# Two products of a recurrent step, alternated block by block, with the pieces of x passed through DRAM

## What is computed

```
def cell(h, x):
    gi = x @ W_ih + b_ih
    gh = h @ W_hh + b_hh
    r, z = sigmoid(i_r + h_r), sigmoid(i_z + h_z)
    n = tanh(i_n + r * h_n)
    return (1 - z) * n + z * h
hs = scan(cell, cond, x over T)
y = x + ffn(hs)     # gate, up, silu, down; each operand rounded to fp8
```

## Time and profile before

| what | value |
|---|---|
| median of three runs | 3157.83 us |
| span of the profiled execution, first to last instruction | 3161.0 us |
| TensorE busy | 2796.5 us (88% of the span) |
| VectorE busy | 1810.4 us (57%) |
| GpSimd busy | 1223.7 us |
| ScalarE busy | 1176.4 us |
| time given to the change's stages (0 to 2305.2 us) | 73% of the span |

### The profile page before, as it was taken

The page is one execution under the profiler, slowest core; times in us unless marked ns, Lnnn a source line. Parts: engine busy times, 40 slices in busy tenths (PEclk is TensorE's granted clock), DMA queues, the critical chain, the costliest instruction groups (busy, mean ns, idle before and its releaser), DMA issues. The chain is left out here.

```text
span 3161.0 us, 156688 instructions
## 1 busy us (share of the span) xinstructions
PE 2796.5 (88%) x67963; PEld 1879.9 (59%) x67963; DVE 1810.4 (57%) x3503; ACT 1176.4 (37%) x2417; POOL 1223.7 (39%) x600
## 2 busy tenths in 40 slices
PE   5799999999988989999999999999921699999996
PEld 2378876887776868887767655647410244444442
DVE  8635223522488634426739154270966488888887
ACT  2422222222211122225609122130345477777774
POOL 0156555655544545652160523416020133333333
PEclk9899999999999999999999999999965899999998
DMA  7812222222212212223454442424240222332221
GB/s 218 275 52 65 62 60 55 64 63 56 57 52 54 59 47 62 66 61 93 139 132 141 125 135 91 133 79 139 87 158 28 87 78 81 91 87 84 85 74 49
DMA packets 212035, 286.41 MB, mean 91 GB/s; under 512 B 46893, under 2 KB 171847, under 8 KB 211719
## 3 DMA queue, kind: packets, MB, share of 16 engines
q1 hardware_dynamic: 194663, 235.99, 26.6%
q10 hardware_dynamic: 13568, 33.56, 3.0%
q0 software_dynamic: 3680, 15.21, 1.7%
HBM read 226.10 MB, written 58.48 MB: 90 GB/s over the span
## 5 line engine op out<-in xcount | busy, mean ns | idle before, releaser
L871 PE MATMUL psum<-whole_w,whole_hot 64*32 64x384 f16 x32768 | 1206.7, 326 | 40.8 <-issue 17.0
L879 PE MATMUL psum<-low_w,low_hot 64*32 64x384 f16 x16384 | 1009.7, 326 | 3.5 <-issue 3.5
L871 PEld LDWEIGHTS psum<-whole_w,whole_hot 64*32 64x32 f16 x32768 | 743.4, 92 | 200.9 <-DVE whole_w L1053 52.2
L753 POOL TENSOR_TENSOR low_hot<-low_a,sum_mask 128x1024 f16<-128x1024 f16 x256 | 485.2, 1895 | 534.3 <-DVE low_a L1041 433.0
L747 POOL TENSOR_TENSOR whole_hot<-whole_a,whole_mask 128x2048 f16<-128x2048 f16 x128 | 462.4, 3612 | 581.0 <-PE psum L871 511.6
L1053 DVE TENSOR_SCALAR whole_w<-psum 32x384 f16<-32x384 f32 x496 | 272.2, 549 | 702.2 <-PE psum L871 694.2
L821 ACT ACTIVATE whole_w<-psum 32x384 f16<-32x384 f32 x496 | 239.3, 482 | 969.8 <-PE psum L871 966.9
L941 PE MATMUL psum<-low_w,low_hot 64*64 64x384 f16 x12288 | 507.2, 325 | 9.5 <-ACT low_hot L839 7.9
L941 PEld LDWEIGHTS psum<-low_w,low_hot 64*64 64x64 f16 x12288 | 372.6, 108 | 143.3 <-ACT low_hot L839 8.4
L879 PEld LDWEIGHTS psum<-low_w,low_hot 64*32 64x32 f16 x16384 | 406.8, 92 | 61.6 <-issue 8.2
L1828 PE MATMUL psum<-wh,hT 128*64 128x256 f32 (+1 forms) x1856 | 315.2, 492 | 0.0
(11 more groups left out here) (265 smaller groups left out, 3086.0 us busy)
## 6 DMA issues: line engine op xcount, KB each, us to landing
low_w<-w_rows SPq DMA_DIRECT2D x384, 144.0 KB, 2.5
low_w<-w_rows SPq DMA_DIRECT2D x256, 120.0 KB
whole_w<-w_rows SPq DMA_DIRECT2D x1024, 24.0 KB, 1.8
x_gates<-x_out ACTq DMA_DIRECT2D x58, 384.0 KB, 2.4
xg<-x_gates SPq DMA_DIRECT2D x58, 384.0 KB, 3.2
low_w<-w_rows SPq DMA_DIRECT2D x256, 72.0 KB
low_w<-w_rows SPq DMA_DIRECT2D x384, 48.0 KB, 2.3
w_rows<-w_split SPq DMA_DIRECT2D x24, 384.0 KB, 6.5
```

The lines of the kernel that those rows point to most:

```text
L753: nc.gpsimd.tensor_tensor(low_hot[:, buf].rearrange("p (s k) b -> p s k b", s=SUBS), low_a[:, bass.ds(c, 1), :, :].rearrange("p a s b -> p ...
L871: last = nc.tensor.matmul(run[m][u][j * Q:(j + 1) * Q, :], whole_hot[rows[u], buf, sign, kk, j % 2 * Q:(j % 2 + 1) * Q], whole_w[rows[u], ...
L879: nc.tensor.matmul(run[m][u][j * Q:(j + 1) * Q, :], low_hot[rows[u], buf, kk, j % 2 * Q:(j % 2 + 1) * Q], low_w[rows[u], buf, at:at + UC], ...
```

## The change

The products now stand in `STAGES`: {(0,0), (0,1)}, {(2,0)}, {(1,0), (1,1)}, {(3,0)}, {(2,1)}, {(3,1)}, {(4,1)}, {(5,1)}. In a stage of two, blocks of x and of the state alternate: block c of x, block c of the state, block c+1 of x, and so on. Each product has one of the two buffers. Both column halves take every term together, so a block has 16 terms. A base is made while the other product's block runs.

The pieces of x for steps 0 to 3 and of the first state no longer pass through `pick`. They are turned in the setup, cut by VectorE, written to a DRAM tensor `pieces` (5 DMAs of 3072 runs of 128 bytes), and read back onto their partitions: 16 DMAs of 8 partitions with 64 runs of 128 bytes each for `low_a`, and 8 with 32 runs for `whole_a`, an operand of a two-level product. For x of step 0 and the first state ScalarE issues them in the setup (48 in all). For x of steps 2, 1 and 3 SyncE issues them between its weight loads (16, 24 and 16).

The plain x sums leave the setup. There are four windows of 7, 7, 7 and 8 pairs, beside the gates of steps 2 to 5. The gates of step 0 run beside (2,0), those of step 1 beside (3,0), none is woven into a two-level product. The load of `w_x` moves from the start of the exact steps to the start of (3,0).

The diff, cut to its core:

```diff
-X_FINE, H_FINE = 2, 2
+FINE = 2
-PRODUCTS = ((0, 0), (0, 1), (1, 0), (1, 1), (2, 0), (2, 1), (3, 0), (3, 1), (4, 1), (5, 1))
-CUT_FROM = 5
+STAGES = (((0, 0), (0, 1)), ((2, 0),), ((1, 0), (1, 1)), ((3, 0),), ((2, 1),), ((3, 1),), ((4, 1),), ((5, 1),))
-SOLO = 3
-WEAVE = 10
-            SETUP_PAIRS = 7
-            WINDOWS = EXACT - X_SUMS + 1
+            WINDOWS = EXACT - FINE
+            pieces = nc.dram_tensor("pieces", [X_SUMS + 1, A_KINDS, D, B], F16, kind="Internal").ap()
+            def put_pieces(eng, operand, split_a):
+                eng.dma_start(pieces[operand].rearrange("a (g p) b -> p a g b", p=P),
+                              split_a.rearrange("p a (g b) -> p a g b", b=B)).then_inc(pieces_out, 16)
+            def load_low(eng, operand, kinds, slot):
+                for r, kind in enumerate(kinds):
+                    for u in range(2):
+                        at = u * B + r * SK
+                        eng.dma_start(low_a[at:at + SK, slot].rearrange("k c s b -> k (c s) b"),
+                                      pieces[operand, kind].rearrange("(n k) b -> k n b", k=SK)).then_inc(rows_of_in[slot], 16)
+            def load_whole(eng, operand, m, slot):
+                ... (2 parts x 2 subs x 2 kinds, 8 partitions with 32 runs each)
 setup, ScalarE, after chunk n of the weights:
-                            if n == 0: ... place_bias, copy_rows
-                            elif n <= SETUP_PAIRS: ... take_out, place_bias, copy_rows
+                            if n == 0:
+                                for j, operand in enumerate((0, H0)):
+                                    a.wait_ge(first_cut, CUTS * (j + 1))
+                                    put_pieces(a, operand, first_split[:, j])
+                            elif n == 1:
+                                a.wait_ge(pieces_out, 32)
+                                for j, (operand, slot) in enumerate(((0, ROWS_X0), (H0, ROWS_H))):
+                                    load_low(a, operand, LOW_ROWS, slot)
+                                    load_whole(a, operand, j, slot)
 setup, VectorE, ahead of the first chunk:
+                        for j, src in enumerate((turned_x[0], turned_h0)):
+                            for _ in cut(v, cut_link, src, scale[:, 2 + j:3 + j], first_rest[:, 0], first_rest[:, 1],
+                                         [first_split[:, j, kind] for kind in range(A_KINDS)]):
+                                pass
 exact steps, SyncE:
+                        for c in range(2):
+                            for m in range(2):
+                                load(0, m, c, m)
+                            if c == 0:
+                                for n, t in enumerate(LATER):
+                                    sp.wait_ge(later_cut, CUTS * (n + 1))
+                                    put_pieces(sp, t, later_split[n])
+                        sp.wait_ge(pieces_out, 16 * (2 + len(LATER)))
+                        load_low(sp, 2, SUM_ROWS, ROWS_X2)
+                        pair_blocks(sp, pair_load(0), 2)
+                        for c in range(BUFS):
+                            load(2, 0, c, sum_buf(c))
+                            if c == 1:
+                                sp.wait_ge(hot_ok, block_no(2, 0, 0) + 1)
+                                load_low(sp, 1, LOW_ROWS, ROWS_X0)
+                                load_whole(sp, 1, 0, ROWS_X0)
+                        sum_blocks(sp, sum_load(2, 0), BUFS, BUFS)
+                        for m in range(2):
+                            load(1, m, 0, m)
+                        sp.wait_ge(hot_ok, block_no(1, 0, 0) + 1)
+                        load_low(sp, 3, SUM_ROWS, ROWS_X2)
+                        store_state(0)
+                        pair_blocks(sp, pair_load(1), 1)
 exact steps, TensorE:
-                                    for kk in range(SOLO):
-                                        term(first + kk, 0)
-                                    based(1, ready)
-                                    for kk in range(SOLO, BK):
-                                        term(first + kk, 0, ((first + kk - SOLO, 1),))
-                                    for kk in range(BK - SOLO, BK):
-                                        term(first + kk, 1)
+                            def term(m, kk):
+                                for u in range(2):
+                                    add_whole(m, u, 1, kk)
+                                for u in range(2):
+                                    add_low(m, u, kk)
+                                for u in range(2):
+                                    last = add_whole(m, u, 0, kk)
+                            with pe.Fori(0, NBK) as c:
+                                for m in range(2):
+                                    ... (waits for bases, weights, one-hots of this block)
+                                    for kk in range(BK):
+                                        term(m, kk)
+                        for t in range(FINE):
+                            if t > 0:
+                                turn(t)
+                                pick(t)
+                            ... (clear)
+                            pair_chain(t)
+                            sum_chain(t + FINE, 0)
+                        for t in range(FINE, EXACT):
+                            turn(t)
+                            ... (clear)
+                            pick(t)
+                            sum_chain(t, 1)
+                            x_window(t)
```

More of the change, by code:

```diff
@@ L643, in renewals, with stage_of, first_block @@
-                def renewals(eng, renew):
-                    with eng.Fori(0, NBK // PAIR - 1) as n:
-                        for b in range(PAIR):
-                            renew(n * PAIR + (b + 1), (b + 1) % PAIR)
-                    renew(NBK - 1, (NBK - 1) % PAIR)
+                def stage_of(t, m):
+                    return next(n for n, stage in enumerate(STAGES) if (t, m) in stage)
+                def first_block(n):
+                    return sum(NBK * len(stage) for stage in STAGES[:n])
@@ new lines, in sum_blocks, with pair_blocks @@
+                def sum_blocks(eng, block, first=0, done=0):
+                    for c in range(done, first):
+                        block(c, sum_buf(c))
+                    with eng.Fori(first // BUFS, NBK // BUFS) as n:
+                        for j in range(BUFS):
+                            block(n * BUFS + j, sum_buf(j))
+                def pair_blocks(eng, block, first, last=NBK):
+                    with eng.Fori(first, last) as c:
+                        for m in range(2):
+                            block(c, m)
@@ new lines, in _ @@
+                        for half in range(2):
+                            sp.dma_start(state[half * B:(half + 1) * B, :], cond[:, half * HALF:(half + 1) * HALF]).then_inc(h0_in, 16)
+                        with nc.allow_non_contiguous_dma(reason="index columns, 6 KB"):
+                            sp.dma_start(dcol[:], dn_idx.rearrange("(c p) -> p c", p=P)).then_inc(dcol_in, 16)
+                        for c in range(2):
[5 more added lines that the diff above has]
+                                    put_pieces(sp, t, later_split[n])
@@ L781, in x_window @@
+                        for j in range(2):
+                            load_rows(a, j)
                         def x_window(t):
@@ L796, in x_window, with place @@
                                     copy_rows(a, n // 2 + 1, WINDOW_BANKS)
+                        def place(t):
+                            for n in range(places(t)):
+                                a.wait_ge(selected, placed_by(t) + n + 1)
+                                group, whole = pick_of(t, n)
+                                if whole:
+                                    last = nc.scalar.activation(whole_a[Q:2 * Q, 1, group::PB, :], picked(n, slice(Q, 2 * Q)), ACT.Copy)
+                                else:
+                                    for part in range(2):
+                                        last = nc.scalar.activation(low_a[part * B:(part + 1) * B, ROWS_H, group::PB, 0, :], picked(n, slice(0, B)), ACT.Copy)
+                                last.then_inc(placed, 1)
@@ L1037, in place_second @@
+                        def place_second(t):
+                            for n in range(places(t)):
+                                v.wait_ge(selected, placed_by(t) + n + 1)
+                                group, whole = pick_of(t, n)
                                 if whole:
-                                    last = nc.vector.tensor_copy(whole_a[B + Q:2 * B, group::PB, :], picked(n, slice(B + Q, 2 * B)))
+                                    last = nc.vector.tensor_copy(whole_a[B + Q:2 * B, 1, group::PB, :], picked(n, slice(B + Q, 2 * B)))
@@ L1383, in build @@
+                        for t in range(FINE, EXACT):
+                            cut_state(t)
+                            place_second(t)
```

(4 more changed lines are left out.)

663 lines of the change are left out of this document (321 added, 342 removed).

## The result

| | before | after |
|---|---|---|
| median of the runs, us | 3159.05 (3154.62 to 3167.09) | 3081.42 (3077.94 to 3084.92) |
| ratio, 95% interval | | 0.9747 (0.9729 to 0.9766) |
| span of the profiled execution, us | 3161.0 | 3078.3 |

2.5% faster; 3027 us was forecast, in a range of 2960 to 3115. Of the experiments' executions one, of e2_lag_back, took 4275.01 us at a granted clock of 0.642 (its nine others 0.929 to 0.931), and no ratio uses it. Against the span that the prediction added up, 3030.1, the profile is 48.2 us longer. First the windows of the profile after, cut where TensorE changes from one stage to the next. Columns: stretch in us, its length, busy time of each engine with its instructions, granted clock of TensorE as a share of full speed, mean busy share of the 16 DMA engines, GB/s.

A forecast was written before the change was run, and what follows sets the result against it. TensorE's chain of products and gaps bounds the kernel. 187.4 + 38.1 + 63.9 + 9 - 82.2 - 2 = 214.2 us gained, less 83.3 for small DMAs, takes span 3161.0 to 3030.1, median 3027 us; range 2960 to 3115.

The forecast's parts named there:

- p: Time one DMA of 512 runs of 128 bytes holds its issuing queue: 1.15 us taken, ends 0.5 and 4.1.
- Part 1, no lag: Two-level products: a block falls from 19 steps to 16, 9.27 to 7.81 us, 187.4 us gained over 128 blocks.
- weights can't keep 7.81: Rival, pair blocks: weight loads come late, a block takes 8.3 us, 64 us more, 3091 us; chance 0.08.
- at 0.52 a block is 8.3 us: Rival, pair blocks: steps with two halves don't keep 0.49 us when they follow one another, about 3091 us; chance 0.04.
- Part 2, the order: Gains between and within products: 38.1 us from woven gates, 63.9 from gaps, 9 from two starts fewer.
- Part 3, the x sums: Setup gets back nearly nothing; step 2's gates need their own window, 82.2 us lost; w_x load ahead of (3,0), 2 lost.
- Part 4, DRAM: Pieces' DMAs in setup, first stage, (2,0) and second stage: 92p - 22.5, 83.3 us lost.
- cheap rival: Small runs cost no more than the issue, p = 0.5: 24 us lost, 2968 us; chance 0.22.
- 20p - 7.9: Loss in (2,0) from 24 DMAs of pieces ahead of block 2's weight load: 15.1 us.
- 14 us for sharing engines with w_rows: Setup: ScalarE, held 40p by its 48 DMAs, is held 14 us more by nine writes of w_rows.
- dear p: Rival: small runs as dear as behind dcol beside w_x, p = 2.2: 180 us lost, 3123 us; chance 0.12.
- slower rival: ScalarE and SyncE held until small runs have landed, p = 4.1, setup first: 355 us lost, 3298 us; chance 0.06.

The follow-up runs named there:

- e2_lag_back: The kernel after with half 1 of each block again three terms behind half 0 (19 steps), TensorE alone changed: 3170.94 us, ratio to before 1.0024.
- e3: The kernel before with the lag set to 0, blocks of one product still following each other: 3326.85 us, ratio to before 1.0527.
- e4: The kernel after with 7 waits instead of 9 at a pair block's start, low weights' wait moved behind 16 matmuls: 3068.16 us, ratio to before 0.9713.
- e7: The kernel after with seven pairs of plain x sums back in the setup, 22 left for the four windows: 3068.57 us, ratio to before 0.9703.
- e8: The kernel after with the pair products' loop written out twice (4 blocks in its body) on TensorE: 3638.65 us, ratio to before 1.1501.
- e1: The kernel after with the pair products' loop written out four times (8 blocks in its body) on TensorE: 3552.15 us, ratio to before 1.1248.
- e5: The kernel after with low rows' DMAs reading 8 runs of 8192 bytes instead of 512 short ones, same bytes: 3045.29 us, ratio to before 0.9619.

## Why the prediction was right, and by how much its terms were off

| term | forecast, us | measured, us | miss |
|---|---|---|---|
| end of the setup | 191 | 177.7 | -13.3 |
| setup's end to first pair block | 14.1 | 14.5 | +0.4 |
| first stage | 521 | 549.0 | +28.0 |
| (2,0) | 101.2 | 100.5 | -0.7 |
| turn, cut and pick ahead of the second stage | 18 | 22.9 | +4.9 |
| second stage | 506 | 528.7 | +22.7 |
| (3,0), (2,1) with their gaps | 189.2 | 194.4 | +5.2 |
| four windows against three and the gates | 82.2 | 83.3 | +1.1 |

The 189.2 is what the prediction leaves of before: a gap of 0.5, 86.0 for (3,0), 2 for the load of w_x, a gap of 14.0, and 86.7 for (2,1) (the window 1570.20:1656.90 of before).

The range was right and so was the sign. But 3081.42 us lies above the forecast's own part of the range, 2995 to 3078, though p came out at 1.1, and two of the prediction's own signs stand against each other: the setup with VectorE idle for 35 to 45 us and the two holes came, and so did "blocks over 8 us", which it lists under wrong. That the sum ended only 48 us off is luck in part: the setup was put 13.3 us too high and the pair stages 50.7 too low.

Point by point:

- **Part 1, no lag: right in sign, mis-sized, and the largest miss.** "16 steps at 0.488, 7.81 us, if the supplies keep up": steps and supplies are as forecast, but at a boundary TensorE waited for itself. The same branch, register operations and waits stand in before, at steps of one half; the prediction took 9.27 us there as 19 steps and nothing else. The rows of before hold two errors that cancel: across a block's change half 1's last low pass (shown below the list) and half 0's first one, 320.85 in the earlier trace rows, are 0.71 us apart, 0.22 more than a step, and half 1 ends 1.21 us behind half 0, 0.25 less than three steps. By the windows, parts 1 and 2 gave 128.0 us, with 17.8 us of holes of the first stage in them, where 187.4 and 9 for the starts were claimed. e2 shows that the split was wrong too: 41 us are the order's, 87 the lag's once the order is there, and by e3 the lag's removal alone is a loss. The rival "weights can't keep 7.81" named this size of block, 8.3 us, and another cause; e4 speaks against that cause. The rival "at 0.52 a block is 8.3 us" named it too, and the steps of 0.49 us speak against that one.
- **Part 2, the order: right.** No gates in a pair stage, a gap of 0.4 us ahead of (2,0). The gap ahead of the second stage was put 4.9 us too low. The one ahead of (3,0) is 5.1 us, not 0.5 and 2 for w_x: TensorE waits 4.6 us for `low_hot`, which ScalarE begins at 1396.13, behind the four issues of w_x.
- **Part 3, the x sums: right for the windows, 83.1 us each.** That the setup gets "nearly nothing" back holds less well once ScalarE and its DMAs fill it: in e7 the pairs cost it 17 us.
- **Part 4, DRAM: right in size, in part by luck.** p was 1.04 to 1.25 for 1.15, a value taken as the middle of two that differ by a factor of four. In the first stage DMAs cost 10.7 and 4.4 us for 15.7, but the 4.4 are behind the three writes of pieces, for which the sum has no term: by it the loads ahead of the 16 DMAs end 21.3 us into the stage, and they ended at 31.7. (2,0) has 15.5 for 15.1, the second stage none for 2.0. The hole of 2.7 us, by the instructions' first fetch, was in no term either. One slip in the cheap rival: by 20p - 7.9 its (2,0) costs 2.1 us, not 4.1. The 14 us for sharing engines with w_rows in the setup did not appear: 48 DMAs held ScalarE 43.2 us, not 46 + 14. That term, drawn from bytes at 245 GB/s, was the other mis-sized one (ScalarE came to them at 78.5 instead of 72, and was let go 10 us sooner than reckoned); with it the setup hid a quarter of the first miss.

The row for part 1, of before:

```profile
320.14 0.35 PE L879 MATMUL psum<-low_w,low_hot 64*32 64x384 f16 x4
```

The low p and the dear p are both refuted. The slower rival is as well: ScalarE was let go as soon as its 48 issues were through.

## What to carry to other kernels

A lag that covers a dependence can cost less than its steps (here 0.68 us for three steps of 0.49), because its ragged ends overlap and hide the boundary's own instructions; price its removal with the boundary laid bare, here about 0.1 us for each two semaphore waits and 0.5 us for a loop end. Many small DMAs behind one another hold the engine that issues them: give them out between its other work, or to the queue with slack, before changing anything else. Count writes as well as reads when DMAs are put into a queue. Before writing a loop out, multiply its instructions by 64 bytes: 98 KB stayed here, 197 KB was fetched in every pass.

## What the runs showed of the hardware, unexpected

- A loop body on TensorE of 1536 matrix instructions (98 KB) runs from what is held; one of 3072 is fetched in each pass, at 555 us / 417 = 1.3 us lost for each 16 KB (e8; 466 / 386 = 1.2 in e1).
- The branch at the loop's end is 208 ns in the median. The Trainium skill, Advanced Engine Details and Errata, section "Control Flow Timing", gives about 108 ns for a compare-and-branch; the row decides.
- DMAs of 8 partitions with runs of 8192 bytes (e5) and of 128 bytes (after), stretches of 16 such DMAs:

```profile
205.00:210.00 5.00, 5.00 (x216) 3.40 (x208) 0.00 (x0) 0.00 (x0) 0.00 (x0) 0.82 0.50 97
```
```profile
99.00:117.00 18.00, 0.00 (x0) 0.00 (x0) 0.00 (x0) 0.00 (x0) 0.00 (x0) 0.50 0.75 56
```

The busy share rises from 0.50 to 0.75 while the rate falls from 97 to 56 GB/s. The share is the packets' summed time over that of 16 engines, and packets overlap: up to 29 are under way at once in the trace of after. So 0.75 doesn't count engines.

The Trainium skill, DMA: Bandwidth & Descriptors, section "Why a DMA increments its semaphore by 16 and not by 1", would put a DMA of 8 partitions on 8 of 16 engines. The trace agrees: besides their data the 48 DMAs of the setup leave 384 packets of 4 bytes in ScalarE's queue, 8 for each, and the two writes of 128 partitions ahead of them 32, 16 for each. The doubled value that the prediction set beside its sum, 1.2 us, is also nearer to the 1.04 to 1.25 measured than the 0.6 it was doubled from. That the number of engines is the reason was not tried.
